# Row maxima of a two-pass softmax turned by another engine, and scratch queries laid out for one transfer per group of heads

## The reference, cut to what matters

```python
def attention(q, k, v, Wq, Wk, Wv, Wfc, bfc):
    qh = (q @ Wq.T).reshape(N, S, 32, 16).transpose(0, 2, 1, 3)
    kh = (k @ Wk.T).reshape(N, S, 8, 16).transpose(0, 2, 1, 3)    # repeated 4 times
    vh = (v @ Wv.T).reshape(N, S, 8, 16).transpose(0, 2, 1, 3)    # repeated 4 times
    score = einsum('bhqd,bhkd->bhqk', qh, kh) / 4
    out = einsum('bhqk,bhkd->bhqd', softmax(score), vh)
    return out.reshape(N, S, 512) @ Wfc.T + bfc

x = x + tanh(g_xattn) * attention(layernorm(x), ctx, ctx, ...)
x = x + tanh(g_ffn) * ffn(layernorm(x))     # shared 2048 wide, routed 256 wide, top 2 of 8 experts
```

## Time and profile before

| | |
|---|---|
| median of 3 executions | 888.61 us |
| lowest, highest | 887.78, 889.78 us |
| the profiled execution, its own time | 890.05 us |
| its span, first to last instruction | 887.7 us |
| mean granted TensorE clock | 0.99 |
| busy: PE, DVE, ACT, POOL | 860.1, 635.8, 337.2, 477.8 us |

### The profile page before, as it was taken

The page is one execution under the profiler, slowest core; times in us unless marked ns, Lnnn a source line. Parts: engine busy times, 40 slices in busy tenths (PEclk is TensorE's granted clock), DMA queues, the critical chain, the costliest instruction groups (busy, mean ns, idle before and its releaser), DMA issues.

```text
span 887.7 us, 14887 instructions
## 1 busy us (share of the span) xinstructions
PE 860.1 (97%) x4923; PEld 642.5 (72%) x4923; DVE 635.8 (72%) x1085; ACT 337.2 (38%) x636; POOL 477.8 (54%) x485
## 2 busy tenths in 40 slices
PE   8689999999999889999999999999999999999998
PEld 6445665665565447888888888888788888888886
DVE  7789899889889966666556655679665566656565
ACT  4186576667657852122112211344211121112111
POOL 2313004001203999787668666954966696678640
PEclk9889999999999999999999999999999999999999
DMA  7763342432432113121112111211311112111102
GB/s 274 232 175 105 127 121 61 149 116 78 131 107 74 38 28 93 48 72 47 47 47 71 47 47 47 72 47 65 115 59 48 47 52 66 47 47 47 47 1 95
DMA packets 43609, 71.88 MB, mean 81 GB/s; under 512 B 6064, under 2 KB 21936, under 8 KB 43312
## 3 DMA queue, kind: packets, MB, share of 16 engines
q1 hardware_dynamic: 43568, 71.34, 25.5%
HBM read 55.33 MB, written 15.73 MB: 80 GB/s over the span
## 4 chain that ended last, share of the span: by engine, by line
PE 84%; DVE 11%; issue 2%; ACT 1%; DMA 1%; SPq 0%; DVEq 0%; ACTq 0%
PE bank L1293 24%; PE bank L1295 23%; PE bank L1294 23%; DVE mcol L906 5%; PE bank L1353 4%; PE bank L1378 4%; PE bank L1368 3%; PE bank L1298 2%; PE bank L1399 1%; DVE oN L1038 1%; ACT probs L761 1%; DVE oB L1028 1%; DVE x_l L1256 1%; DVE aT_l L881 0%; DMA q_scr<-qx_l 0%
## 5 line engine op out<-in xcount | busy, mean ns | idle before, releaser
L1293 PE MATMUL bank<-x_l,w_h 128*128 128x512 f32 x504 | 197.3, 391 | 0.3 <-DVE c L1116 0.3
L1294 PE MATMUL bank<-x_h,w_l 128*128 128x512 f32 x504 | 196.2, 389 | 0.0
L1295 PE MATMUL bank<-x_h,w_h 128*128 128x512 f32 x504 | 196.2, 389 | 0.0
L906 DVE TENSOR_REDUCE mcol<-bank 128x2 f32<-128x512 f32 x256 | 164.7, 671 | 24.8 <-PE bank L1353 24.3
L620 ACT ACTIVATE hT_h<-bank 128x512 fp32r<-128x512 f32 x72 | 43.1, 599 | 355.9 <-DVE bank L1231 347.2
L761 ACT ACTIVATE probs<-bank 128x512 f32<-128x512 f32 x256 | 138.9, 596 | 73.3 <-PE bank L1368 71.7
L572 POOL TENSOR_TENSOR w_l<-raw,w_h 128x512 fp32r<-128x512 f32 (+1 forms) x144 | 161.9, 1157 | 2.9
L1128 DVE SCALAR_TENSOR_TENSOR xa<-bank,tgf,xa 128x512 f32<-128x512 f32 x128 | 96.2, 751 | 77.7 <-PE bank L1295 77.5
L1293 PE MATMUL bank<-dn_l,hT_h 128*128 128x512 f32 x288 | 112.0, 389 | 0.0
L1294 PE MATMUL bank<-dn_h,hT_l 128*128 128x512 f32 x288 | 112.0, 389 | 0.0
L1295 PE MATMUL bank<-dn_h,hT_h 128*128 128x512 f32 x288 | 112.0, 389 | 0.0
(11 more groups left out here) (149 smaller groups left out, 1340.6 us busy)
## 6 DMA issues: line engine op xcount, KB each, us to landing
raw<-w_gu SPq DMA_DIRECT2D x36, 512.0 KB, 3.3
dnraw<-w_dn SPq DMA_DIRECT2D x36, 256.0 KB, 2.6
q_st<-q_scr SPq DMA_DIRECT2D x64, 128.0 KB, 2.7
q_scr<-qx_h SPq DMA_DIRECT2D x16, 256.0 KB, 2.2
q_scr<-qx_l SPq DMA_DIRECT2D x16, 256.0 KB, 2.2
q_st<-q_scr SPq DMA_DIRECT2D x64, 64.0 KB, 2.7
out<-xa SPq DMA_DIRECT2D x16, 256.0 KB, 2.0
cx_raw<-ctxT SPq DMA_DIRECT2D x14, 256.0 KB, 3.0
```

The source lines that it names most:

```text
L906: v.tensor_reduce(at[:, :, qt], sm_bank(n, s, u)[:, :].rearrange("p (r k) -> p r k", r=2), AX.X, ALU.max).then_inc(max_ok, 1)
L1293: mm(out, a_h, b_l, start=start, stop=False, skip_group_check=onto)
L1294: mm(out, a_l, b_h, start=False, stop=False, skip_group_check=onto)
L1295: return mm(out, a_h, b_h, start=False, stop=stop, skip_group_check=onto)
```

## The change

1. Turning the maxima. `mt_job` on PE and `m_copy` on ScalarE are gone. `mcol` has 32 columns for each of two steps; VectorE transposes them in blocks of 32 x 32 (`turn_maxima`), right behind the first maximum (u = 0) of a step, for step n+1. It has one more memset at the start. The minus sign goes into the ones of `k_st`, now -1. `mT` and the semaphore `m_rd` are doubled.
2. Sending them. `put_max` has four DMAs instead of two, each of sixteen 128-byte pieces, and stands first in SyncE's step, ahead of `read_q`, the loads of the context and `write_k`.
3. Layout. `q_scr` and `k_scr` hold three parts in the order of the operand's rows. Each half of a chunk is one DMA of 48 partitions: two in place of four. The high part of the queries is written twice: three writes in place of two. The keys keep three writes.
4. Waits for `mt_cp` and for `ob_ok` at `mt_job` are gone from PE; counts of the semaphores follow.

```diff
             def write_q(tb, oc):
-                for part, (done, tile) in enumerate(((q_hi, qx_h), (q_lo, qx_l))):
+
+                for part, done, tile in ((0, q_hi, qx_h), (2, q_hi, qx_h), (1, q_lo, qx_l)):
                     sp.wait_ge(done, CHUNKS * tb + oc + 1)
                     sp.dma_start(q_scr[tb, oc, :, part, :], r(tile[:, oc % 2, :])).then_inc(q_wr[oc], 16)
...
             def read_q(tb, bb, c, n, fresh):
...
                 for e in range(2):
                     at, rows, tok = e * ROWS, slice(e * ROWS, (e + 1) * ROWS), slice(bb * S, (bb + 1) * S)
-                    sp.dma_start(r(q_st[at:at + 2 * DH, c, :, :]),
+                    sp.dma_start(r(q_st[at:at + SM, c, :, :]),
                                  q_scr[tb, c, rows, :, tok].rearrange("(h d) a q -> (d a) h q", d=DH)).then_inc(q_rd[c], 16)
-                    sp.dma_start(r(q_st[at + 2 * DH:at + 3 * DH, c, :, :]),
-                                 q_scr[tb, c, rows, 0, tok].rearrange("(h d) q -> d h q", d=DH)).then_inc(q_rd[c], 16)
...
             def put_max(n, slot):
-                sp.wait_ge(mt_cp, n + 1)
-                for e in range(2):
-                    at = e * ROWS + MROW
-                    sp.dma_start(r(q_st[at:at + 1, slot, :, :].rearrange("p h (t q) -> p (h t) q", q=P)),
-                                 r(mT[e * HC:(e + 1) * HC, :])).then_inc(m_rd, 16)
+                sp.wait_ge(mt_ok, n + 1)
+                for j in range(4):
+                    lot = 32 * j
+                    sp.dma_start(r(q_st[MROW:MROW + ROWS + 1:ROWS, slot, :, :].rearrange("e h (t j q) -> e (h t) j q",
+                                                                                       j=4, q=32)[:, :, j, :]),
+                                 r(mT[lot:lot + 16, slot % 2, :])).then_inc(m_rd[slot % 2], 16)
...
                 for s in range(STEPS):
                     n = STEPS * t + s
+                    if not last or s + 1 < STEPS:
+                        put_max(n + 1, (s + 1) % CHUNKS)
                     if s + 3 < STEPS or not last:
...
                     if s == 4 and not last:
                         write_k(t + 1)
-                    if not last or s + 1 < STEPS:
-                        put_max(n + 1, (s + 1) % CHUNKS)
...
-            def m_copy(n):
-
-                act.wait_ge(mt_tr, n + 1)
-                if not (isinstance(n, int) and n == 0):
-                    act.wait_ge(m_rd, 32 * n)
-                nc.scalar.activation(mT[:, :], OTB[0:16, 0:P], ACT.Copy, scale=-1.0).then_inc(mt_cp, 1)
...
+            def turn_maxima(n, par):
+
+                dve.wait_ge(max_ok, UNITS * (n + 1))
+                if not (isinstance(n, int) and n < 2):
+                    dve.wait_ge(m_rd[par], 32 * (n - par))
+                v.transpose(mT[:, par, :].bitcast(f32),
+                            mcol[:, par, :].bitcast(f32)).then_inc(mt_ok, 1)
...
-            v.memset(k_st[:, :, :, :].bitcast(f32), 1.0).then_inc(consts, 1)
+            v.memset(k_st[:, :, :, :].bitcast(f32), -1.0).then_inc(consts, 1)
+            v.memset(mcol[:, :, :].bitcast(f32), 0.0)
...
             for u in range(UNITS):
                 maximum(1, 1, u, 1)
+                if u == 0:
+                    turn_maxima(0, 0)
...
                             maximum(n + 2, (s + 2) % STEPS, u, s % 2)
+                        if u == 0 and (not last or s + 1 < STEPS):
+                            turn_maxima(n + 1, (s + 1) % 2)
...
-            def mt_job(n, par):
-
-                pe.wait_ge(max_ok, UNITS * n + UNITS)
-                if not (isinstance(n, int) and n < 2):
-                    pe.wait_ge(ob_ok, n - 1)
-                tr(OTB[0:16, 0:P], mcol[:, par, :]).then_inc(mt_tr, 1)
...
-            pe.wait_ge(q_lo, 3)
-            mt_job(0, 0)
...
                         if v == 0:
-                            pe.wait_ge(m_rd, 32 * (n + 1))
+                            pe.wait_ge(m_rd[s % 2], 32 * (n - s % 2) + 64)
                         st_pair(n, v, bb, c)
...
-                            if not last or s + 1 < STEPS:
-                                pe.wait_ge(mt_cp, n + 2)
                             for p in (0, 1):
                                 pv_unit(n, p, bb, c)
...
-                        if v == 1 and (not last or s + 1 < STEPS):
-                            pe.wait_ge(mt_cp, n + 1)
-                            mt_job(n + 1, (s + 1) % 2)
```

More of the change, by code:

```diff
@@ L46, in build @@
     ALU, ACT, AX = mybir.AluOpType, mybir.ActivationFunctionType, mybir.AxisListType
-    q_scr = nc.dram_tensor("q_scr", (BLOCKS, CHUNKS, P, 2, BLOCK), f32, kind="Internal").ap()
-    k_scr = nc.dram_tensor("k_scr", (BLOCKS, P, 2, BLOCK), f32, kind="Internal").ap()
-    kl_scr = nc.dram_tensor("kl_scr", (BLOCKS, P, BLOCK), f32, kind="Internal").ap()
+    q_scr = nc.dram_tensor("q_scr", (BLOCKS, CHUNKS, P, 3, BLOCK), f32, kind="Internal").ap()
+    k_scr = nc.dram_tensor("k_scr", (BLOCKS, P, 3, BLOCK), f32, kind="Internal").ap()
     with ExitStack() as ctx:
@@ L115, in build @@
         tbias = sb("tbias", [P, D], f32, att)
-        mcol = sb("mcol", [P, 2, 16], f32, att)
-        mT = sb("mT", [16, P], f32r, att)
+        mcol = sb("mcol", [P, 2, 32], f32r, att)
+        mT = sb("mT", [P, 2, 32], f32r, att)
         rden = sb("rden", [P, 16], f32, att)
@@ L169, in build @@
         q_wr = [sem(f"q_wr{c}") for c in range(CHUNKS)]
-        k_wr, kl_wr = sem("k_wr"), sem("kl_wr")
+        k_wr = sem("k_wr")
         q_rd = [sem(f"q_rd{c}") for c in range(CHUNKS)]
         k_rd = [sem("k_rd0"), sem("k_rd1")]
-        m_rd = sem("m_rd")
+        m_rd = [sem("m_rd0"), sem("m_rd1")]
         stored = sem("stored")
@@ L188, in build @@
         sm_full, st_full, max_ok = [sem("sm_full0"), sem("sm_full1")], [sem("st_full0"), sem("st_full1")], sem("max_ok")
-        mt_tr, mt_cp = sem("mt_tr"), sem("mt_cp")
+        mt_ok = sem("mt_ok")
         exp_ok, pv_ok = sem("exp_ok"), sem("pv_ok")
@@ L295, in write_k @@
                 sp.wait_ge(k_lo, tb + 1)
-                for part in range(2):
-                    sp.dma_start(k_scr[tb, :, part, :], r(kx_h[:, :])).then_inc(k_wr, 16)
-                sp.dma_start(kl_scr[tb, :, :], r(kx_l[:, :])).then_inc(kl_wr, 16)
+                for part, tile in enumerate((kx_h, kx_h, kx_l)):
+                    sp.dma_start(k_scr[tb, :, part, :], r(tile[:, :])).then_inc(k_wr, 16)
             def read_q(tb, bb, c, n, fresh):
@@ L655, in q_high @@
                     if oc >= 2:
-                        act.wait_ge(q_wr[oc - 2], 32)
+                        act.wait_ge(q_wr[oc - 2], 48)
                 else:
-                    act.wait_ge(q_wr[(oc + 2) % 4], 32 * (tb + 1) if oc >= 2 else 32 * tb)
+                    act.wait_ge(q_wr[(oc + 2) % 4], 48 * (tb + 1) if oc >= 2 else 48 * tb)
                 copy(qx_h[:, oc % 2, :], q_bank(tb, oc)[:, :]).then_inc(q_hi, 1)
@@ L721, in _ @@
             act.wait_ge(wkv_ok, 1)
-            m_copy(0)
             def a_high(n, c, bb, batch):
@@ L763, in body @@
                                              ACT.Exp, scale=float(DH) ** -0.5).then_inc(exp_ok, 1)
-                        if u == 3 and (not last or s + 1 < STEPS):
-                            m_copy(n + 1)
                         if u == 5 and not (first and s == 0):
@@ L1431, in _ @@
             q_job(3)
-            pe.wait_ge(k_rd[0], 64)
-            pe.wait_ge(q_rd[0], 64)
+            pe.wait_ge(k_rd[0], 32)
+            pe.wait_ge(q_rd[0], 32)
             for v in range(UNITS // 2):
                 sm_pair(0, 0, v, 0, 0)
-            pe.wait_ge(q_lo, 3)
-            mt_job(0, 0)
-            pe.wait_ge(q_rd[1], 64)
+            pe.wait_ge(q_rd[1], 32)
             for v in range(UNITS // 2):
```

23 lines of the change are left out of this document (8 added, 15 removed).

## The result

| | before | after |
|---|---|---|
| median of 8 executions each | 888.64 us | **894.56 us** |
| lowest, highest | 887.78, 889.81 | 892.40, 896.92 |
| ratio of the two, 95% interval | | 1.0062 [1.0053, 1.0072] |
| profiled execution: own time, span | 890.05, 887.7 | 894.77, 893.0 |
| mean granted TensorE clock in it | 0.99 | 0.985 |

The kernel became slower by 5.9 us, outside the predicted range (884.3 to 890.6), on the side of rival C.

What follows compares the result with a forecast made beforehand. Only attention could move, its chain alternating between PE and VectorE. Terms -2.8 + 1.8 - 0.3 + 0.3 - 0.2 = -1.2 us took the median 888.61 to 887.4 us; range for 8 in 10: 884.3 to 890.6.

Steps and rivals of the forecast that it cites:

- rival C: SyncE's queue becomes late behind four DMAs of maxima, deciding from 0.65 us per DMA on: sum +2.5, 891.1 us; chance 0.14.
- What bounds the kernel: In attention the chain of waits alternates between PE and VectorE; maxima ready 2 us sooner are worth nothing.
- PE's turns, -2.8: 32 turns leave PE: 0.11 us each in 18 steps, 2.0 us, plus 0.8 for a removed wait in step 30.
- VectorE's turns, +1.8: 32 turns come to VectorE: 0.16 us each in the eleven steps where it holds the chain, +1.8 us.
- Rival D: VectorE becomes the bound in more steps at 0.45 us a turn: sum +3.3, 891.9 us; chance 0.05.
- ScalarE, -0.3: 32 copies of 266 ns leave ScalarE, covered by its idle time except in the first steps: -0.3 us.
- SyncE late at s = 5, +0.3: Blocks 0 to 2: last query read, behind the maxima, met or missed by a tenth; +0.1 each, +0.3 us.
- rival B: Earlier reads end PE's wait sooner and cut the prologue's low clock short, about 4 us: 883.4 us; chance 0.06.
- Prologue, -0.2: Fewer read DMAs and no `mt_job(0)` between early scores, against extra query writes: about -0.2 us, bounds -2 and +2.

Runs made afterwards that it cites:

- e9: Kernel before, with PE's turn of the maxima done twice into the same place: 891.33 us, ratio 1.0024 to the kernel before.
- e8: Kernel before with the turn moved to VectorE, old order and layout, plus a second VectorE transpose into an unread tile: 888.68 us, ratio 0.9996.
- e1: Kernel before with only the turn of the maxima moved to VectorE, old order and layout: 887.39 us, ratio 0.9983.
- e12: Kernel before with the turn on VectorE, and the next block's first queries written before the keys are read at s = 4: 886.91 us, ratio 0.9976.
- e6: The whole change, but at s = 4 the next block's first queries are written before the keys are read: 889.24 us, ratio 1.0003.
- e5: The whole change, but in step s = 4 alone the four maxima stand behind the keys' writes: 889.60 us, ratio 1.0008.
- e10: Kernel before with turn on VectorE and new layout, maxima at their old place, first queries written before keys are read: 888.71 us, ratio 0.9997.
- e3: Kernel before with turn on VectorE and maxima first in SyncE's step, old layout: 889.17 us, ratio 1.0010.
- e11: Kernel before with turn on VectorE, maxima first, old layout, first queries written before keys are read: 889.25 us, ratio 0.9998.
- e2: Kernel before with only the new layout, maxima turned by PE and sent at the old place: 890.25 us, ratio 1.0011.
- e4: The change with the maxima at their old place behind `write_k`, so turn and layout only: 889.60 us, ratio 1.0010.

## Why the prediction was wrong

- **What bounds the kernel: right.** Two engines alternate on the chain, and to have maxima sooner was worth nothing: nobody waits for `mT` before or after.
- **PE's turns, -2.8: 2.0 of it right, 0.8 too high.** A turn costs 0.12 us by doubling, 0.11 predicted, and all 32 cost 1.9 us (e9) for my 2.0. Steps 6, 14 (in kernels without the gap) and 22 went from 9.34 to 9.22. Step 30 went from 7.45 to 7.13, where I had put 0.8 for the removed wait: 0.3 came, and 0.2 of it went back in step 31.
- **VectorE's turns, +1.8: right in kind, too high.** 0.09 us for 0.16, and 1.2 us in all (e8). The row (201 ns) was as read from neighbours, but on the chain it takes less than the reciprocal's 0.16. Rival D (0.45 us) falls.
- **ScalarE, -0.3:** nothing in the profiles speaks for or against so small a term. Together the parts of the turn came to -1.5 us (e1, by its ratio); my sum without SyncE's term was -1.5 as well. That the two are equal is partly luck: PE's term and VectorE's were each too large and make up for each other, and in the profiled executions the steps behind length 4 gave 0.8 us (e1) to 1.4 (e12), the rest coming in the prologue.
- **SyncE late at s = 5, +0.3: the step that failed.** It was +5.2 us (the change against e6). I wrote that the place to watch is s = 5 and that there "it is met or missed by a tenth". The place of the damage was right (scores of steps 6, 14, 22 waiting for `q_st<-q_scr`, the sign of rival C), its cause was not. First, I counted the maxima that pass the reads in s = 5, which cost nothing (e5), and gave no price to those that pass the keys' writes one step earlier. They had been covered by the wait for the keys' landing (160.15 to 161.5, in a wait from 159.70 to 163.13) and lost that cover when they moved ahead of it; my text says of other steps that nothing waits for the reads so soon, and never asks what waits for `write_k`. Second, I kept the landings at 2.2 and 2.7 us, of a machine with less to move. They became 3.3 and 3.4 at this place: 1.8 us on a slack of 1.3. Third, I counted every issue at its usual length, and in blocks 0 and 1 one on the path took 1.51 and 1.31 us.
- **Rival C: the mechanism in substance, wrong in its condition and price.** I said that it decides from 0.65 us per DMA on. A DMA issued in 0.50, and it happened all the same, at 894.6 instead of 891.1.
- **The clock: left out.** I had it only as a gain in the prologue (rival B), and that did not come: the low level lasted 23.9 us there (34.25 to 58.14), for 17.1 before (35.94 to 53.01). Behind the gap of 1.65 us on PE it cost another 1.2 to 1.3 us in step 14. The eight executions differ in the same way: three at a mean granted clock of 0.99 took 892.4 to 893.4 us, five at 0.98 to 0.985 took 894.4 to 896.9.
- **Prologue, -0.2:** as a net it is near (the copy four steps after the first starts at 92.83 us for 92.45, +0.4), but it hides larger terms, each read from single executions: -1.5 to -2.5 from the turn (90.96 in e12, 89.95 in e1), +1.6 from the layout (92.60 in e10), and +2.4 to +3.0 from the order (92.39 in e3, 93.99 in e11), of which the whole change shows little.

## What to carry to other kernels

A wait in an in-order queue is a place where work is free. Before an instruction is moved, look not only at what it passes but at the wait that it leaves: beside the new layout, the four maxima cost 4.8 us by leaving the wait for the keys' landing (e5). Count slack per path, not per edit: on the path of s = 4 layout and order cost about 1 us each one by one, and 5.2 together. And look for the rest elsewhere: the same two edits cost about 2 us more in the prologue and right behind it. And where reads are made fewer by writing more, price the writes by what they do to landings on the path.

## What was not expected of the hardware

- Landings react to what is issued around them. A read of 192 KB took 3.4 to 3.5 us (median) in all kernels with the new layout, where reads of 128 and 64 KB took 2.6 to 2.7 in all others, whatever the order. The 256 KB writes of queries took 2.2 us before, 2.3 to 3.0 with the layout and the old order (e2, e4, e10), 2.5 to 2.6 with the new order and the old layout (e3, e11), and 3.4 to 3.6 with both (the change, e5, e6). So the third write is not the whole of it. Whether size, number or neighbours do it was not taken apart. The Trainium skill, page "DMA: Bandwidth & Descriptors", section "Latency and other measured facts", puts HBM's access at 0.2 us on average and 2 us at high load; the direction agrees with these medians, its figures no run here shows.
- A DMA of sixteen 128-byte pieces issued in 0.50 us, one of eight 512-byte pieces in 0.64 (medians). Now and then a single issue took 1.0 to 2.2 us, in every kernel (1.31 in the chain of the change, 1.90 in that of e3), at times at the very place where it counts.
- Beside gaps on PE the granted clock fell to 1.2 GHz in some executions: for 3.4 us from 1.4 us after the end of a gap of 1.65 (the change, 177.6) or from 0.15 after one of 1.32 (e3, 316.5), and for 10.2 us from 0.5 us before the end of one of 1.39 (e11, 61.0). Shorter gaps had it too (0.90 us ending at 57.72 in e4, low from 57.96). After the gaps of 1.33, 1.23 and 1.32 us at 101.6, 252.3 and 319.2 in the change it stayed at 2.4 GHz. What decides it is open.
